# A fused four-block transformer step: attention scores of the first stage computed in row halves of the matrix array

## The reference

```
qp = (q @ Wq + bq).reshape(B, H, S, hd)          # H = 16, hd = 16: a plain reshape
kp = k @ Wk + bk                                  # one key of 16 features for all heads: 77 x 16
vp = v @ Wv + bv
att = softmax(einsum('bhsd,btd->bhst', qp, kp) / 16)
out = einsum('bhst,btd->bhsd', att, vp)
x = x + tanh(g_xattn[0]) * out
```

## Time and profile before

| | us |
|---|---|
| three runs | 1150.38, 1150.58, 1151.35 (median 1150.58) |
| the profiled execution | 1147.46, of which 1145.7 is the span of the trace |
| first stage in the span | 0 to about 402 |
| 100 to 200 us | PE busy 90.1, PEld 75.3, DVE 88.8, ACT 76.5, POOL 52.8 |

### The profile page before, as it was taken

One profiled execution on the slowest core, in us unless ns is written; L12 is line 12 of the kernel. 1 busy time (PEld: TensorE's weight loads), 2 busy tenths in 40 slices (PEclk: granted clock), 3 DMA queues, 4 the chain that ended last, 5 costly groups with the idle time before them and its releaser, 6 DMA issues. The chain is left out here.

```text
span 1145.7 us, 24403 instructions
## 1 busy us (share of the span) xinstructions
PE 981.6 (86%) x7085; PEld 868.5 (76%) x7085; DVE 855.9 (75%) x2301; ACT 588.9 (51%) x1349; POOL 489.0 (43%) x695
## 2 busy tenths in 40 slices
PE   5889989989998675899999999982779869999973
PEld 3767777777776443799999999972668769999962
DVE  3788998898996343688888888875666747888767
ACT  2577777777776352334343434422545346666520
POOL 3455455455453001345354444433376714444420
PEclk9899999999998776999999999996889989999996
DMA  6674674575560040101011010200333213444357
GB/s 157 148 139 96 141 143 96 122 142 116 112 143 1 0 128 22 49 25 48 24 35 37 24 48 24 93 2 1 101 125 120 89 55 117 125 123 130 106 200 241
DMA packets 85875, 104.44 MB, mean 91 GB/s; under 512 B 15070, under 2 KB 75438, under 8 KB 85808
## 3 DMA queue, kind: packets, MB, share of 16 engines
q1 hardware_dynamic: 77616, 81.91, 28.9%
q0 software_dynamic: 7632, 21.05, 5.1%
q10 hardware_dynamic: 560, 0.66, 0.2%
HBM read 38.50 MB, written 57.62 MB: 84 GB/s over the span
## 5 line engine op out<-in xcount | busy, mean ns | idle before, releaser
L413 POOL TENSOR_TENSOR prob_lo_hi<-prob,prob_lo_hi 128x616 f16<-128x616 f32 x64 | 95.7, 1496 | 126.7 <-ACT prob_lo_hi L491 126.5
L1647 POOL DMA_INDIRECT expert_out<-early_weights,aim x71 | 69.9, 984 | 101.3 <-DVE aim L1976 84.1
L721 PE MATMUL ps_scores<-kblock,qT 128*128 128x308 f32 x256 | 82.8, 448 | 11.1 <-ACT qT L475 5.8
L1638 POOL DMA_INDIRECT sorted_rows<-m_z,slot_i x64 | 72.5, 1133 | 42.4 <-DVE slot_i L1856 24.6
L1185 ACT ACTIVATE f_hidden<-c_hidden,f_b 128x256 f32<-128x256 f32 x128 | 53.7, 471 | 69.3 <-PE c_hidden L1374 69.3
L1372 PE MATMUL c_mlp<-f_w_hi,f_hidden_hi 128*128 128x256 f32 x256 | 80.9, 316 | 3.6 <-DVE f_hidden_lo L1303 3.6
L787 PE MATMUL ps_probT<-ident,prob_lo_hi 128*77 128x128 f32 x512 | 68.9, 279 | 15.4 <-DVE probT L364 12.8
L787 PEld LDWEIGHTS ps_probT<-ident,prob_lo_hi 128*77 128x77 f32 x512 | 59.3, 151 | 28.6 <-DVE probT L364 16.5
L1372 PE MATMUL c_hidden<-y2T_hi,f_w_hi 128*128 128x256 f32 x256 | 77.7, 304 | 0.0
L629 DVE TENSOR_REDUCE mx<-ps_scores 128x8 f32<-128x616 f32 x64 | 50.6, 791 | 32.8 <-PE ps_scores L721 32.8
L1374 PE MATMUL c_hidden<-y2T_hi,f_w_lo 128*128 128x256 f32 x256 | 72.8, 284 | 0.0
(11 more groups left out here) (336 smaller groups left out, 3306.3 us busy)
## 6 DMA issues: line engine op xcount, KB each, us to landing
sorted_rows<-no_row SPq DMA_DIRECT2D x15, 2322.0 KB, 13.4
m_z<-sorted_rows SPq DMA_DIRECT2D x71, 129.0 KB
early_weights<-expert_chunks SPq DMA_DIRECT2D x8, 640.0 KB, 4.2
combT<-combineT_all SPq DMA_DIRECT2D x16, 256.0 KB, 2.3
slT<-slots_all SPq DMA_DIRECT2D x16, 256.0 KB, 2.5
early_weights<-expert_out SPq DMA_DIRECT2D x8, 512.0 KB, 6.3
early_weights<-expert_out POOLq DMA_DIRECT2D x8, 512.0 KB, 6.3
out<-x_all SPq DMA_DIRECT2D x8, 512.0 KB, 3.4
```

Of the source, the lines that this page charges most:

```text
L413: pool.tensor_tensor(prob2[:, u % 2, :, :, 0], prob[:, u % 2], prob2[:, u % 2, :, :, 1], ALU.subtract).then_inc(lo_done.sem, 1)
L721: return pe.matmul(out, lhsT, rhs, start=start, stop=stop)
L1638: pool.indirect_dma_start(out=sorted_rows[:, :], in_=zn[:, s % 3, t, :], in_offset=None, out_offset=bass.IndirectOffsetOnAxis(ap=slot_i[:, ...
L1647: pool.indirect_dma_start(out=expert_out[:, :], in_=xo[:, i % 3, :], in_offset=None, out_offset=bass.IndirectOffsetOnAxis(ap=aim_i[:, i % ...
```

## The change

K's and V's products are cut to what is used: 77 instead of 128 moving columns for K; for V a stationary side of 77 columns instead of 128, and 16 moving columns instead of 128. `kblock` becomes half as wide: partitions 0 to 63 hold groups 0 to 3 in a block diagonal, partitions 64 to 127 groups 4 to 7 in the same 308 columns. A second mask, made once by POOL at the start, says which group a partition has within its half. Each of the two products of a `scores` unit then takes only its half of the partitions on both sides. Banks, output shapes, waits and the order of the list stay as they are; on every engine the instructions stand in the same order as before, apart from the one for the mask.

```
-        kblock = sb("kblock", [P, UG, L])
+        hmask = sb("group_in_half_mask", [P, UG // 2])
+        kblock = sb("kblock", [P, UG // 2, L])
...
+            pool.wait_ge(id_done.sem, 3)
+            pool.tensor_tensor(hmask[:], gmask[:, 0:UG // 2], gmask[:, UG // 2:UG], ALU.add).then_inc(id_done.sem, 1)
...
-            dve.wait_ge(id_done.sem, 3)
+            dve.wait_ge(id_done.sem, 4)
...
-                dve.scalar_tensor_tensor(out=kblock[:], in0=spread(kT[:].rearrange("p (a l) -> p a l", a=1), 1, UG),
-                                         scalar=bk[:, 0:1], in1=spread(gmask[:].rearrange("p (g a) -> p g a", a=1), 2, L),
+                dve.scalar_tensor_tensor(out=kblock[:], in0=spread(kT[:].rearrange("p (a l) -> p a l", a=1), 1, UG // 2),
+                                         scalar=bk[:, 0:1], in1=spread(hmask[:].rearrange("p (g a) -> p g a", a=1), 2, L),
...
-                    mm(psA[:, 0:P], wk[:, k, :], ctxT[:, k, :], k == 0, k == KD - 1)
+                    mm(psA[:, 0:L], wk[:, k, :], ctxT[:, k, 0:L], k == 0, k == KD - 1)
                 for k in range(KD):
-                    last = mm(psA[:, P:2 * P], ctxT[:, k, :], wv[:, k, :], k == 0, k == KD - 1)
+                    last = mm(psA[0:L, P:P + HD], ctxT[:, k, 0:L], wv[:, k, 0:HD], k == 0, k == KD - 1)
...
                 for h in range(2):
-                    last = mm(psS[:, h, 0:UG // 2 * L], qT[:, chunk, tile * P:(tile + 1) * P],
-                              kblock[:, h * UG // 2:(h + 1) * UG // 2, :].rearrange("p g l -> p (g l)"))
+                    rows = slice(h * P // 2, (h + 1) * P // 2)
+                    last = mm(psS[:, h, 0:UG // 2 * L], qT[rows, chunk, tile * P:(tile + 1) * P],
+                              kblock[rows].rearrange("p g l -> p (g l)"))
```

## The result

| | before | after |
|---|---|---|
| median (runs) | 1150.48 (4) | 1123.69 (4; 1120.15 to 1125.78) |
| ratio, with its 95% interval | | 0.9751 [0.9725, 0.9777] |
| profiled execution, its span | 1147.46, 1145.7 | 1120.15, 1118.4 |
| `turn_xu` to `turn_xu` | 21.69 | 20.19 |

What follows compares the result with a forecast made beforehand. A ring of waits among PE, DVE, ACT and POOL bounds the first stage; 21.3 us from 14 turns, 0.36 from the last with scores and 3 before them sum to 24.7: 1150.6 becomes 1126, range 1120 to 1144 (8 in 10).

Steps and rivals of the forecast that it cites:

- The ring: One first-stage turn: waits among PE, DVE, ACT and POOL close into one loop; 21.69 us becomes 20.17.
- The lead: xn's second half on DVE starts 0.07 us before POOL's `low_part` 3, instead of 0.04 late.
- What is late next: Behind xn, ACT's own queue (`q_out`) holds `squares`, which starts at 255.10 and not 256.26: 1.16 us a turn.
- the stall: xn's second half stands still while POOL's `low_part` 3 works; it was to end at 254.79, not 256.15.
- Scores on the ring: `scores` 1 brings 0.18 us; `scores` 2 only the 0.18 DVE has to give; together 0.36 a turn.
- The two borders of a unit: PE's tiling mode switches around a `scores` unit: 0.20 us each, 0.13 before `values`; unit 0.85 to 0.92, not 1.03.
- a ramp: Before the first of the 14 turns, DVE waits directly for seven or eight units: 2.2 to 5 us, taken as 3.
- the slow turn: In the kernel before, the turn from 214.42 to 237.75 took 23.33 us instead of 21.69; the clock fell to 0.50.
- The halves do not run side by side: Rival, chance 0.05: a `scores` unit takes 1.37 us, the stall still goes, 8 us saved in all, 1142.
- POOL still wins the port: Rival, chance 0.21: xn's second half still loses to POOL; a turn loses 0.36 us only, 8.4 in all, 1142.
- the clock: Rival, chance 0.05: clock drops in PE's pauses at each turn's end, 1.64 us each; two a turn give 1172.
- six low stretches: Stretches with the clock at 0.50, 1.64 us each; six decide against the 8.4 us of "POOL still wins the port".

Runs made afterwards that it cites:

- full_height: The changed kernel with each `scores` product taking all 128 rows on both sides, narrow `kblock`, K and V kept: 1135.06 us, 0.9810 of the kernel before.
- wide_kblock: The changed kernel with `kblock` computed 616 wide again, half-row products and narrow K and V kept: 1160.25 us, 1.0031 of the kernel before.
- delay_xn: The changed kernel with one more small DVE instruction between `kblock` and xn: 1152.98 us, 0.9972 of the kernel before.
- no_clamp: The changed kernel with `runit` in one POOL operation, the lower limit of the norm left out: 1121.68 us, 0.9733 of the kernel before.
- comb_later: The changed kernel with `comb_scale` moved in the list to behind `probT_out` 2: 1123.54 us, 0.9733 of the kernel before.
- same_half: The changed kernel with both products of a `scores` unit in rows 0 to 63, so they can't lie side by side: 1142.43 us, 0.9943 of the kernel before.
- wide_filled: wide_kblock with seven idle identity products in PE's two pauses at the end of a turn: 1133.07 us, 0.9861 of the kernel before.

## Why the prediction was right, and what it had wrong

**The ring was the right one.** The turn fell by 1.50 (1.52 forecast), in the parts forecast: 0.20, 0.17 and 1.14 for 0.18, 0.18 and 1.16. full_height and wide_kblock build either half of it alone (both with the narrow K and V, which by themselves bring nothing), and delay_xn shows the mechanism without the block's width.

**POOL against DVE.** The lead came out at 0.065 for 0.07, and DVE won in every turn. This was the term on which most of the gain hung, with a chance of 0.21 for the other side; the runs now have a loss at -0.03 and a win at 0.065. (By single instructions the kernel before was 0.03 late, not 0.04.) One argument for it was wrong: an earlier `low_part` 2 was to widen the lead, but rs is ready 1.34 us behind `scores_out` 3 before and after, and xn waits for it. full_height, where it comes at 0.94, has the lead of 0.29. The Trainium skill's page "SBUF — State Buffer", section "Who interferes with whom", says that whichever issues first blocks the other fully; the trace agrees in both directions, 1.74 us for xn when it is behind, 1.77 for 1.49 for `low_part` when that is, but for the short piece at the start that runs beside the other.

**What is late next** was forecast as `squares` behind `q_out`, and so it is, but that is not what ends the turn. The prediction let the stall go. It did not go: it moved from xn to the next instruction in DVE's queue, `comb_scale`, which the prediction never named. Two chains then end together, over `comb_scale`, probT and `turn_p` 3, and over `low_part` 3, `ru` and xu. The forecast of 12.05 held because the second had been worked out (`low_part` 3 pushed, `ru` just behind it). The first came to the same time by coincidence; no_clamp and comb_later show that each alone is enough to hold the turn.

**Scores on the ring: right sum, wrong terms.** The prediction priced `scores` 1 by PE's occupancy, 1.03 to 0.85. In fact a unit takes 0.72, with 0.09 more in front of it (`turn_xu` to `scores`: 0.49 before, 0.58 in wide_kblock), and what DVE waits for is the result, 0.31 us earlier (1.73 to 1.42 in wide_kblock and comb_later). The late `comb_scale` takes 0.11 of that back through `scores_out` 0, for which `scores` 1 waits. The 0.20 that remain agree with 0.18 only because the two errors cancel: that is luck. DVE's wait for `scores` 1, forecast near 0.8, is gone, since DVE itself comes late. So in the whole turn the half-row products bring 0.49 by wide_kblock, or 0.44 by full_height, and not 0.36; the narrow block brings 1.06 or 1.01, and not 1.16. The two borders of a unit cost the 0.20 in its 0.72 and the 0.09 ahead of it, 0.29 in all, where the prediction had 0.33 to 0.40. The Trainium skill's page "TensorEngine Tiling (Array Packing)", section "Key Properties", says that changing the tiling mode drains the engine; the trace agrees, with this 0.29 as the size.

**The sum lacked a term.** The forecast took off 24.7 us, the profiled executions differ by 27.3. Its own terms brought 23.5: 21.0 in the 14 turns for 21.3; a ramp of 2.2 (the 3.7 up to the first `turn_xu` less the first turn's 1.5) and not 3, the low end of its bounds; in the last turns 0.44 less 0.14, for 0.36. The other 3.7 are clock: 1.6 for the slow turn that is gone, which the prediction had in its range only, and 2.1 behind the last `turn_xu`, for which it had nothing. So 1126 lies 2.3 us above the median because of what it left out, and not because of the ring.

**The rivals' prices.** "The halves do not run side by side" was 1142, and same_half measured 1142.43 (0.9943, which is 1144 of 1150.6). "POOL still wins the port" was 1142 too, but wide_kblock, which is this rival, measured 1.0031, which is 1154 of 1150.6. The turn had been priced well (21.33; it is 21.20). What failed there is that the clock was a rival by itself and not a part of this one: the prediction let it decide against this rival from six low stretches, and here five turns were long. They cost 3.4, 3.2, 3.2, 2.6 and 1.5 us over 21.20, up to twice the 1.64 assumed and 13.8 together. wide_filled, without them, has its last `turn_xu` at 372.26 instead of 389.43 us, 17.2 earlier; the other 3.4 are 0.08 in each turn and 2.3 in the last one. With the pauses filled the two kernels stand at 0.9861 and 0.9945, whose quotient of 0.9916 is 1141 of 1150.6 (by the two intervals, about 1136 to 1145). So without the clock this rival's 1142 was right. With 0.21 on it, the upper end of the range, 1144, stood 10 us too low.

That the changed kernel had no low stretch from 60 to 340 us fits the reason given, that its last pause was gone; no run takes that pause away by itself, so this is not shown. What PE waits at the end of a turn adds up to 2.27 us in wide_kblock (five long turns), 1.75 before (one) and 1.28 in the changed kernel (none).

What stays open is why the lowered clock comes in some turns and not in others: wide_kblock's turns are alike to 0.07 us where the clock is full, and 5 of 13 lose it. The clock behind the last `turn_xu` was not held fixed in any pair of runs either; that it makes the 2.1 us is read from the stretches listed with the result. It is open, too, why POOL's rs comes 0.4 us later with half-height products.

## What to carry to other kernels

When a stall comes from two engines that contend, ask which instruction is next in the loser's queue: it inherits the stall, however small it is, and can be moved behind something that doesn't need the port. Price a shared port by order of start, in hundredths of a microsecond, and look at what pushes either side. And when a change shortens the work of PE without shortening the wait behind it, look at the clock: filling a pause with idle products is a cheap test that tells a slow kernel from a slow clock.

## What the runs showed of the hardware that was not expected

- A two-column `tensor_scalar` on DVE stood 1.46 us (0.22 otherwise) while POOL's 616-column instruction ran; a 1024-column copy out of PSUM ran beside the same instruction at full speed (1.22).
- 0.1 us of start time, in an instruction of 0.48 us, decided over some 2% of the whole kernel (delay_xn 0.9972 against 0.9751 and 0.9761 for the kernel that it changes), by way of the port and then the clock.
- Half-height float32 products of 308 columns pair fully: in the changed kernel the first pass of each half starts at 237.537 and 237.544 us. In the same rows of the array the same four passes took 0.51 us more.
- Seven products without use took 1.7% off a kernel whose PE had lost clock in its pauses, and 0.5% off one that had lost it in one turn and behind the last scores.
